# One of the values' four products moves into the ranks' step, and the keys' drain ahead of an exponential

## Chip, cores and metric

One core of a Trainium2 chip. The metric is device time of one execution in microseconds (us), as the median of several runs. TensorE is PE below, VectorE DVE, ScalarE ACT, GpSimd POOL, SyncE SP.

## What is computed

x has 8 x 1024 tokens of 128 features, adj is a 1024 x 1024 mask. All in float32.

```python
# attention layer on y = layernorm(x): 4 heads of 32 features
q, k, v = y @ Wq.T + bq, y @ Wk.T + bk, y @ Wv.T + bv
scores = clip(q @ k / sqrt(32), -10, 10);  scores = where(mask == 0, -10, scores)
# keys stand in 8 chunks of 128; the softmax is taken inside each chunk
ctx = sum over chunks of softmax(scores[chunk]) @ v[chunk]
x = x + (layernorm(ctx @ Wo.T + bo + y) * gamma + beta)
# expert layer: 8 experts, the two best per token, hidden size 256
g = layernorm(x);  best two of (g @ Wg + bg)
out = x + sum over the two of (gelu(g @ W1[e] + b1[e]) @ W2[e] + b2[e])
```

## The kernel before

The tokens are cut into 16 blocks of 512 (u = 0 to 15; two blocks make one batch element). A block goes through 8 steps, one for each chunk of 128 keys (j = 0 to 7; s = 8u + j numbers them all, 128 steps). Each engine has its own program, in which the order is written out by hand; semaphores join them.

In each step PE makes the scores of the chunk for the 4 heads (`scores`, L455: 32 rows of the array for each head, into four PSUM banks, which are there once only), then the context and the sums of the exponentials of the chunk two steps back (`context`, L467 and L474: 32 columns each), and then at most a few jobs for other blocks. The scores wait for the semaphore `clipped` of the step before, as the clip on DVE (`clip`, L1029) reads the same banks. Behind the clip ACT takes the exponential (`exponentials`, L779) of the whole step, in place in a ring `e` of three buffers, and DVE turns the context (L1037).

The jobs of PE in block u, behind the step's `context`: step 0 transposes of normalised x2 of block u-3 (`turn_xn2`, L515); step 1 its gate (L530) and half of the output projection of block u-2 (`project`, L565 and L566); step 2 the other half; step 3 transposes of normalised x of block u+2 (`turn_xn`, L486); step 4 the keys of u+2 (`keys`, L494, one fp32 product of 128 x 512); step 5 the ranks of the tokens of u-3 among their expert pairs (`rank`, L538 to L554, small bf16 products); step 6 the values of u+2 (`values`, L503, four fp32 products of 128 x 128, one for each tile of 128 tokens); step 7 the queries of u+2 (`queries`, L508). A product in fp32 stands in the trace as two matmul passes. `rank` has work from block 3 on; keys, values and queries of u+2 in these steps from block 1 to block 13 (block 0 has an order of its own). The last two blocks have no such products, and behind block 15 come the experts' tiles, in which ranks (L538 to L554) and expert products (L617, L631, L657) stand side by side on PE.

Keys and values of a block go through the same PSUM bank: `values` writes to it once the keys have been drained (semaphore `k_ready`). The drains are ACT's work. Its order in a block, each behind the exponential of its step: step 0 the transposes of x2 (L866); step 1 normalising x (L784); step 2 squares of the projection (L817); step 3 the transposes of x (L832, L842) and the normalising of the projection (L824); step 4 the drain of the keys (`drain_k`, L848) and sums of x of block u+3 (L800); step 5 squares of x (L808); step 6 the drain of the values (`drain_v`, L854); step 7 normalising x2 (L784) and the drain of the queries (L860). The transposes of the next block's step 0 wait for that normalising.

Of the kernel before, what the change touches and what calls it, by code (L numbers as in the profile page):

```python
# [21 lines left out]
TILES = BLOCK // P  # L22
# [58 lines left out]
def need(eng, sem, value):  # L81
    if value > 0:
        eng.wait_ge(sem, value)
# [12 lines left out]
def is_block(u):  # L96
    return 0 <= u < BLOCKS


def done(u):  # L100

    return min(max(u + 1, 0), BLOCKS)


def graph_transformer_layer(nc, x, adjT, wqT, bq, wkT, bk, wvT, bv, wo, bo, gamma, beta,
                            wg, bg, w1, b1T, w2, b2, out):
    ctx = ExitStack()
    with ctx:
# [3 lines left out]
        def sem(name):  # L112
            return ctx.enter_context(nc.semaphore(name))
# [129 lines left out]
        def v_ps(v):  # L243
            return job_ps[1] if v == 1 else job_ps[0]
# [70 lines left out]
        v_filled, v_ready = sem("v_filled"), sem("v_ready")  # L315
# [129 lines left out]
        def _(pe):  # L445
# [48 lines left out]
                pe.matmul(k_ps(v)[:], w_proj[:, W_K, :], xnT[:, v % 2, :], start=True, stop=True)\  # L494
                    .then_inc(k_filled, 1)

            def values(v):
                pe.wait_ge(k_ready, v + 1)
                if v == 0:
                    pe.wait_ge(xnT_bo_ready, 1)  # L500
                for t in range(TILES):
                    cols = slice(t * P, (t + 1) * P)
                    ins = pe.matmul(v_ps(v)[:, cols], xnT[:, v % 2, cols], w_proj[:, W_V, :], start=True, stop=True)  # L503
                ins.then_inc(v_filled, 1)

            def queries(v):
                need(pe, v_ready, v + 1 if v else 0)
# [26 lines left out]
            def rank(v):  # L534
                pe.wait_ge(one_hot_ready, v + 1)
                need(pe, n2_ready, done(v + 1))
                to = job_ps[1][:, 0:(TILES + 1) * NP].rearrange("p (t n) -> p t n", n=NP)
                pe.matmul(to[:, 0:TILES, :], tri[:], one_hot[:], start=True, stop=False, skip_group_check=True)  # L538
                pe.matmul(to[:, TILES, :], all_ones[:], one_hot[:, TILES - 1, :], start=False, stop=False,
                          skip_group_check=True)  # L540
                for t in range(TILES - 1):
                    pe.matmul(to[:, t + 1:TILES + 1, :], all_ones[:],
                              one_hot[:, t:t + 1, :].to_broadcast([P, TILES - t, NP]),
                              start=False, stop=False, skip_group_check=True)
                if v == 0:
                    pe.wait_ge(ranks_begun, 1)
                for part, n in enumerate((ROOM - 1, 1)):
                    ins = pe.matmul(to[:, 0:TILES, :], all_ones[0:n, :],
                                    first_rows[0:n, part:part + 1, :].to_broadcast([n, TILES, NP]),
                                    start=False, stop=v == 0 and part == 1, skip_group_check=True)  # L550
                if v > 0:
                    for part in range(2):
                        before = totals[:, (v - 1) % 2, part:part + 1, :]
                        ins = pe.matmul(to[:], all_ones[0:1, :], before.to_broadcast([1, TILES + 1, NP]),  # L554
                                        start=False, stop=part == 1, skip_group_check=True)
                ins.then_inc(rank_filled, 1)
# [124 lines left out]
            for u in range(BLOCKS):  # L681
                for j in range(CHUNKS):
                    s = u * CHUNKS + j
                    scores(s)
                    if s == LAG:
                        pe.wait_ge(consts_ready, 1)
                    if s >= LAG:
                        context(s - LAG)
                    if u == 0:
                        if j == 0:  # L690
                            values(0)
                            keep_busy(7, ctx_ps[:, 0:P])
                        if j == 1:
                            turn_xn(1)
                            keep_busy(6, ctx_ps[:, 0:P])
                        if j == 2:
                            keys(1)
                        if j == 3:
                            turn_xn(2)
                        if j == 4:  # L700
                            values(1)
                        if j == 5:
                            keys(2)
                            queries(1)
                        if j == 6:
                            values(2)
                        if j == 7:
                            queries(2)
                    last = u == LAST
                    if j == 0 and is_block(u - 3):  # L710
                        turn_xn2(u - 3)
                    if last and j == 0:
                        columns(0)
                    if j == 1 and is_block(u - 3):
                        gate(u - 3)
                    if j in (1, 2) and is_block(u - 2):
                        project(u - 2, range(2 * j - 2, 2 * j))
                    if j == 3 and u > 0 and is_block(u + 2):
                        turn_xn(u + 2)
                    if j == 4 and u > 0 and is_block(u + 2):  # L720
                        keys(u + 2)
                    if j == 6 and u > 0 and is_block(u + 2):
                        values(u + 2)
                    if j == 7 and u > 0 and is_block(u + 2):
                        queries(u + 2)
                    if j == 5 and is_block(u - 3):
                        rank(u - 3)
                    if u == LATE and j == 3:
                        offset_columns()
                    if last and j == 3:  # L730
                        ends(0)
                    if last and j == 7:
                        lookup(0)
# [41 lines left out]
        def _(act):  # L775
            def exponentials(s):
                act.wait_ge(clipped, s + 1)
                every = e[:, s % E_RING]
                nc.scalar.activation(every, every, ACT.Exp, scale=SCORE_SCALE).then_inc(exp_done, 1)  # L779
# [65 lines left out]
            def drain_k(v):  # L845
                act.wait_ge(k_filled, v + 1)
                need(act, clipped, CHUNKS * 2 * (v // 2 - 1))
                nc.scalar.activation(kT[v // 2 % 2][:, v % 2 * BLOCK:(v % 2 + 1) * BLOCK], k_ps(v)[:], ACT.Identity,  # L848
                                     bias=bk_sb[:, 0:1]).then_inc(k_ready, 1)
# [68 lines left out]
            for u in range(BLOCKS):  # L918
                for j in range(CHUNKS):
                    s = u * CHUNKS + j  # L920
                    exponentials(s)
                    if u == 0:
                        if j == 1:
                            drain_xnT(1)
                        if j == 2:
                            drain_k(1)
                            normalise_x(2)
                        if j == 3:
                            drain_xnT(2)
                        if j == 4:  # L930
                            drain_v(1)
                        if j == 5:
                            drain_k(2)
                            drain_q(1)
                        if j == 6:
                            drain_v(2)
                        if j == 7:
                            drain_q(2)
                    if j == 0 and is_block(u - 3):
                        drain_xn2T(u - 3)  # L940
                    if j == 1 and u > 0 and is_block(u + 2):
                        normalise_x(u + 2)
                    if j == 2 and is_block(u - 2):
                        square_proj(u - 2)
                    if j == 3 and u > 0 and is_block(u + 2):
                        drain_xnT(u + 2)
                    if j == 3 and is_block(u - 2):
                        normalise_proj(u - 2)
                    if j == 4 and u > 0 and is_block(u + 2):
                        drain_k(u + 2)  # L950
                    if j == 4 and is_block(u + 3):
                        sum_x(u + 3)
                    if j == 5 and is_block(u + 3):
                        square_x(u + 3)
                    if j == 6 and u > 0 and is_block(u + 2):
                        drain_v(u + 2)
                    if j == 7 and is_block(u - 2):
                        normalise_x2(u - 2)
                    if j == 7 and u > 0 and is_block(u + 2):
                        drain_q(u + 2)  # L960
# [676 lines left out]
```

## Time and profile before

| | |
|---|---|
| median of 3 runs | 727.55 us (727.47 to 728.11) |
| profiled execution | 729.22 us, span 727.5 us from first to last instruction |
| granted TensorE clock, mean | 0.992 |
| busy share of the span | PE 95%, PE weight load 50%, DVE 81%, ACT 74%, POOL 78% |
| costliest lines | exponential L779 245.1 us, clip L1029 293.2 us, sums L474 133.3 us |

How to read it: PE and its weight loads are pipelined, and the ends of matmuls are modelled, so starts are the firmer numbers; a busy PE is not PE at its peak. Times in rows are from the start of the span. The chain is the work that ended last, followed back from the last instruction, each step to what released it.

### The profile page before, as it was taken

What the parts mean: (1) busy time and instruction counts of PE and PEld (TensorE: products, weight loads), DVE (VectorE), ACT (ScalarE), POOL (GpSimd) and SP (SyncE); (2) the same over time, 40 slices, a digit from 0 to 9 for tenths busy, and PEclk for the clock granted to TensorE, in tenths of its full rate; (3) what the DMA queues carried; (4) which work ended last, traced back from release to release, by engine and by line L of the source; (5) the groups of instructions that cost most, each with busy time, mean ns of one, the idle gap of its engine ahead of it and who ended that gap; (6) DMA issues with size and microseconds to landing.
All of it is one profiled execution on the core that took longest, in us unless ns stands there. A gap on an engine that the chain in (4) does not pass through costs nothing.

```text
span 727.5 us, 17325 instructions
## 1 busy us (share of the span) xinstructions
PE 689.7 (95%) x5510; PEld 364.0 (50%) x5510; DVE 590.7 (81%) x1270; ACT 538.6 (74%) x1225; POOL 564.9 (78%) x627
## 2 busy tenths in 40 slices
PE   8997999999999999999999999989888999999994
PEld 6421333333333333333333333323378899999994
DVE  4789989898999989999998999999897655555552
ACT  4776787888878788887888887666676566667662
POOL 7759696989889898988988889898776776545553
PEclk9999999999999999999999999999999999999997
DMA  7450010010100101111010010013241354333300
GB/s 259 157 167 30 1 30 15 17 45 30 45 34 27 45 15 45 45 31 45 16 45 23 27 43 15 30 54 108 62 130 55 97 157 125 97 96 102 105 26 2
DMA packets 47961, 45.45 MB, mean 62 GB/s; under 512 B 6981, under 2 KB 42576, under 8 KB 47872
## 3 DMA queue, kind: packets, MB, share of 16 engines
q1 hardware_dynamic: 41888, 31.60, 15.5%
q0 software_dynamic: 5984, 12.74, 5.0%
q8 instruction: 47, 0.77, 0.5%
q14 instruction: 42, 0.34, 0.2%
HBM read 27.73 MB, written 18.34 MB: 63 GB/s over the span
## 4 chain that ended last, share of the span: by engine, by line
PE 69%; DVE 15%; issue 6%; ACT 5%; DMA 1%; DVEq 1%; SPq 1%; POOLq 0%; POOL 0%; ACTq 0%
PE scores_ps L455 15%; PE ctx_ps L467 11%; DVE e L1029 10%; PE scores_ps L631 9%; PE z_ps L474 9%; PE ctx_ps L657 5%; PE z_ps L657 5%; ACT x_rows L784 3%; PE job_ps L503 2%; PE job_ps L530 2%; PE job_ps L494 2%; PE job_ps L566 2%; ACT e L779 1%; PE job_ps L515 1%; PE job_ps L565 1%
## 5 line engine op out<-in xcount | busy, mean ns | idle before, releaser
L779 ACT ACTIVATE e<-e 128x2048 f32<-128x2048 f32 x128 | 245.1, 1915 | 109.3 <-DVE e L1029 108.5
L1029 DVE SCALAR_TENSOR_TENSOR e<-scores_ps,bound_mem 128x2048 f32<-128x2048 f32 x128 | 293.2, 2290 | 40.0 <-PE scores_ps L455 34.6
L901 ACT ACTIVATE e<-scores_ps,bound_mem 128x128 f32<-128x128 f32 x364 | 104.4, 374 | 51.0 <-PE scores_ps L631 51.0
L1533 POOL DMA_INDIRECT out<-e,near x91 | 91.0, 1000 | 62.0 <-DVE e L1253 49.0
L474 PE MATMUL z_ps<-e,one_column 128*32 128x512 f32 x1024 | 133.3, 592 | 0.0
L1514 POOL TENSOR_TENSOR ctx_part<-ctx_part,z_inv 128x1024 f32<-128x1024 f32 x60 | 115.5, 1925 | 18.2 <-DVE z_inv L1045 18.1
L1526 POOL TENSOR_TENSOR ctx_sum<-ctx_sum,ctx_part 128x512 f32<-128x512 f32 x90 | 115.7, 1285 | 8.4 <-POOL ctx_sum L1526 0.9
L631 PE MATMUL scores_ps<-e,bound_mem 128*128 128x128 f32 x728 | 97.0, 276 | 4.0 <-ACT e L872 2.1
L1037 DVE STREAM_TRANSPOSE ctx_part<-ctx_ps 128x512 f32<-128x512 f32 x128 | 90.3, 705 | 1.6 <-PE ctx_ps L467 1.6
L631 PEld LDWEIGHTS scores_ps<-e,bound_mem 128*128 128x128 f32 x728 | 88.5, 192 | 5.6 <-ACT e L872 3.9
L1488 POOL DMA_INDIRECT sorted_rows<-x_rows,slot x64 | 63.5, 993 | 19.3 <-issue 16.1
L474 PEld LDWEIGHTS z_ps<-e,one_column 128*32 128x32 f32 x1024 | 33.4, 110 | 76.5 <-issue 76.2
L467 PE MATMUL ctx_ps<-e,v_last 128*32 128x512 f32 x512 | 68.2, 604 | 1.4 <-DVE ctx_part L1037 1.3
L467 PE MATMUL ctx_ps<-e,near 128*32 128x512 f32 x512 | 68.2, 605 | 0.0
L1236 DVE TENSOR_TENSOR bound_mem<-near,b_pair 128x128 f32<-128x128 f32 x91 | 28.8, 316 | 41.9 <-issue 40.2
L455 PE MATMUL scores_ps<-near 32*128 32x512 f32 x320 | 45.6, 639 | 4.9 <-DVE e L1029 4.5
L657 PE MATMUL ctx_ps<-bound_mem,e 128*128 x368 | 48.9, 275 | 0.5 <-DVE e L1253 0.5
L455 PE MATMUL scores_ps<-near,k_last 32*128 32x512 f32 x320 | 45.6, 639 | 3.8 <-DVE e L1029 3.4
L657 PE MATMUL z_ps<-bound_mem,e 128*128 x360 | 47.7, 275 | 1.1 <-DVE e L1253 1.1
L657 PEld LDWEIGHTS ctx_ps<-bound_mem,e 128*128 128x128 f32 x368 | 44.8, 192 | 0.8 <-issue 0.7
L657 PEld LDWEIGHTS z_ps<-bound_mem,e 128*128 128x128 f32 x360 | 43.8, 192 | 1.4 <-issue 1.3
L1227 DVE COPY bound_mem<-bound_mem 128x258 f32 x170 | 43.4, 298 | 0.2 <-issue 0.2
(194 smaller groups left out, 1055.8 us busy)
## 6 DMA issues: line engine op xcount, KB each, us to landing
near<-sorted_rows SPq DMA_DIRECT2D x91, 130.0 KB, 2.2
near<-in_x SPq DMA_DIRECT2D x16, 256.0 KB, 2.8
bound_mem<-in_adjT SPq DMA_DIRECT2D x4, 1024.0 KB, 10.0
x_post<-in_x SPq DMA_DIRECT2D x16, 256.0 KB, 2.7
sorted_rows<-pad_row SPq DMA_DIRECT2D x1, 3640.0 KB, 15.3
out<-e,near POOLq DMA_INDIRECT x91, 2.3
sorted_rows<-x_rows,slot POOLq DMA_INDIRECT x64
bound_mem<-in_w SPq DMA_DIRECT2D x1, 1024.0 KB, 5.7
```

The lines of the kernel that those rows point to most:

```text
L455: ins = pe.matmul(scores_ps[:, h, :], kT[u // 2 % 2][rows_of, j * P:(j + 1) * P], qT[u % 3][rows_of, :], start=True, stop=True)
L467: ins = pe.matmul(ctx_ps[rows_of, :], v_sb[u // 2 % 2][:, j, rows_of], e[:, s % E_RING, h, :], start=True, stop=True)
L474: ins = pe.matmul(z_ps[rows_of, :], one_column[:, j, :], e[:, s % E_RING, h, :], start=j == 0, stop=j == CHUNKS - 1, skip_group_check=True)
L631: ins = pe.matmul(scores_ps[:, i % 2, k * P:(k + 1) * P], part_flat[:, at:at + P], xT, start=True, stop=True)
L657: ins = pe.matmul(to, e_flat[:, h_at:h_at + P], w_out[:, bass.ds(ways_out[i][k // 2], D)], start=k == 0, stop=k == 3)
L779: nc.scalar.activation(every, every, ACT.Exp, scale=SCORE_SCALE).then_inc(exp_done, 1)
L901: nc.scalar.activation(e_flat[:, h_at:h_at + P], scores_ps[:, i % 2, k * P:(k + 1) * P], ACT.Gelu, bias=part_flat[:, bias_at:bias_at + 1]) ...
L1029: dve.scalar_tensor_tensor(out=e[:, s % E_RING], in0=scores_ps[:], scalar=-CLIP, in1=to, op0=ALU.max, op1=ALU.min).then_inc(clipped, 1)
L1037: dve.transpose(ctx_part[:, s % PARTS, :, :].rearrange("p a b -> p (a b)"), ctx_ps[:])\
L1514: nc.gpsimd.tensor_tensor(pair, pair, z_inv[:, v % 2, j:j + 2].to_broadcast([P, 2, SQUARES, DH]), ALU.mult).then_inc(ctx_scaled, 1)
L1526: nc.gpsimd.tensor_tensor(to, first, ctx_part[:, at], ALU.add).then_inc(ctx_added, 1)
L1533: nc.gpsimd.indirect_dma_start(out=out_rows, out_offset=bass.IndirectOffsetOnAxis(ap=near_u[:, id_at:id_at + 1], axis=0), in_=e_flat[:, at ...
```

## The change

On PE `values` gets a list of tiles. The product of the first tile of block u+2 is made in step 5, behind the ranks of block u-3 (in blocks 1 and 2, which have no ranks there, behind the step's sums); the other three stay in step 6, and the last of them signals `v_filled` as before. Both groups begin with the wait for `k_ready`. On ACT the drain of the keys of u+2 is put ahead of the exponential of step 4, where it stood behind it. Blocks 1 to 13 are touched.

```diff
-            def values(v):
+            def values(v, tiles=range(TILES)):
                 pe.wait_ge(k_ready, v + 1)
                 if v == 0:
                     pe.wait_ge(xnT_bo_ready, 1)
-                for t in range(TILES):
+                for t in tiles:
                     cols = slice(t * P, (t + 1) * P)
                     ins = pe.matmul(v_ps(v)[:, cols], xnT[:, v % 2, cols], w_proj[:, W_V, :], start=True, stop=True)
-                ins.then_inc(v_filled, 1)
+                if TILES - 1 in tiles:
+                    ins.then_inc(v_filled, 1)
...
                     if j == 6 and u > 0 and is_block(u + 2):
-                        values(u + 2)
+                        values(u + 2, range(1, TILES))
                     if j == 7 and u > 0 and is_block(u + 2):
                         queries(u + 2)
                     if j == 5 and is_block(u - 3):
                         rank(u - 3)
+                    if j == 5 and u > 0 and is_block(u + 2):
+                        values(u + 2, range(1))
...
                     s = u * CHUNKS + j
+                    if j == 4 and u > 0 and is_block(u + 2):
+                        drain_k(u + 2)
                     exponentials(s)
...
-                    if j == 4 and u > 0 and is_block(u + 2):
-                        drain_k(u + 2)
                     if j == 4 and is_block(u + 3):
                         sum_x(u + 3)
```

## Rows read from the trace of the kernel before

**Rows 1.** The page, parts 1 and 4: busy time by engine; the chain by engine.

```profile
PE 689.7 (95%) x5510; PEld 364.0 (50%) x5510; DVE 590.7 (81%) x1270; ACT 538.6 (74%) x1225; POOL 564.9 (78%) x627
...
PE 69%; DVE 15%; issue 6%; ACT 5%; DMA 1%; DVEq 1%; SPq 1%; POOLq 0%; POOL 0%; ACTq 0%
```

**Rows 2.** The chain in block 10, from step 4 on: start us, us, what.

```profile
350.46 1.06 PE job_ps L494 x2
...
355.04 0.12 PE job_ps L554 x2
355.16 1.05 PE scores_ps L455 x8
...
358.06 1.09 PE job_ps L503 x8
...
360.36 2.30 DVE e L1029
...
362.69 0.46 ACT e L779
...
364.50 1.65 ACT x_rows L784 x4
...
366.19 0.66 PE job_ps L515 x4
```

**Rows 3.** Timeline of DVE, block 10, clips of steps 5, 6: start, us, [idle before].

```profile
352.72 2.29 DVE L1029 SCALAR_TENSOR_TENSOR e<-scores_ps,bound_mem 128x2048 f32<-128x2048 f32 x1 [0.70 <-PE scores_ps L455]
...
356.35 2.29 DVE L1029 SCALAR_TENSOR_TENSOR e<-scores_ps,bound_mem 128x2048 f32<-128x2048 f32 x1
```

**Rows 4.** Timeline of PE, last rank matmul and next scores, blocks 10 and 4.

```profile
354.94 0.22 PE L554 MATMUL job_ps<-totals,all_ones 1*128 1x140 bf16 x1
355.07 0.71 PE L455 MATMUL scores_ps<-near,k_last 32*128 32x512 f32 x4
...
166.56 0.22 PE L554 MATMUL job_ps<-totals,all_ones 1*128 1x140 bf16 x1
166.69 0.71 PE L455 MATMUL scores_ps<-near 32*128 32x512 f32 x4
```

**Rows 5.** Timeline of PE, block 10, step 6: sums, values' passes, next scores.

```profile
357.02 1.04 PE L474 MATMUL z_ps<-e,one_column 128*32 128x512 f32 x8
358.00 0.38 PE L503 MATMUL job_ps<-w_proj,near 128*128 128x128 f32 x1
...
358.21 0.50 PE L503 MATMUL job_ps<-w_proj,near 128*128 128x128 f32 x3
...
358.88 0.28 PE L503 MATMUL job_ps<-w_proj,near 128*128 128x128 f32 x1
359.08 0.71 PE L455 MATMUL scores_ps<-near,k_last 32*128 32x512 f32 x4
```

**Rows 6.** Timeline of PE, block 2, step 5: sums, then the next scores.

```profile
102.22 1.04 PE L474 MATMUL z_ps<-e,one_column 128*32 128x512 f32 x8
103.89 1.14 PE L455 MATMUL scores_ps<-near,k_last 32*128 32x512 f32 x8 [0.63 <-DVE e L1029]
```

**Rows 7.** Timeline of PE in the experts' part: rank(13), then an expert product.

```profile
532.45 0.22 PE L554 MATMUL job_ps<-totals,all_ones 1*128 1x140 bf16 x1
532.60 0.38 PE L657 MATMUL z_ps<-bound_mem,e 128*128 x1
...
532.82 0.50 PE L657 MATMUL z_ps<-bound_mem,e 128*128 x3
```

**Rows 8.** Timeline of ACT, block 10, steps 4 to 6: exponentials and the keys' drain.

```profile
351.22 1.95 ACT L779 ACTIVATE e<-e 128x2048 f32<-128x2048 f32 x1
353.02 0.72 ACT L848 ACTIVATE near<-job_ps,bk_sb 128x512 f32<-128x512 f32 x1
...
355.05 1.91 ACT L779 ACTIVATE e<-e 128x2048 f32<-128x2048 f32 x1 [0.15 <-DVE e L1029]
...
358.68 1.91 ACT L779 ACTIVATE e<-e 128x2048 f32<-128x2048 f32 x1 [0.17 <-DVE e L1029]
```

## Prediction, made before the changed kernel was run

> **What bounds the kernel now.** Page first: PE is busy 95% of the span and carries 69% of the chain that ended last, DVE 15%, ACT 5% [rows 1]. All of the edit lies in the 13 blocks u = 1 to 13, so next I read the chain inside one of them (block 10; the others repeat it) [rows 2]. From the keys' product in step 4 to the end of step 6 it stays on PE without a break: scores, context, sums, the step's job, next scores. Only behind the scores of step 7 does it leave PE: clip 2.30 us on DVE, the exponential and the normalising of x2 on ACT, then back to PE for that tile's transposes in the next block's step 0. So whatever moves the scores of step 7 moves the whole next block by the same amount; nothing in the chain between absorbs it.
>
> Then each step was asked what releases its scores: the end of the clip before (scores overwrite the banks that the clip reads) or PE's own queue. In step 5 both come together. The clip runs 352.72 to 355.01 [rows 3]; the next scores start at 355.07, 0.06 after it, and 0.13 after the start of the last rank matmul [rows 4]. Block 4 shows the same 0.13, and so do all the blocks 4 to 13 (in block 3 the records of these two matmuls are missing). In step 6 the clip ends at 356.35 + 2.29 = 358.64 [rows 3], but the next scores start at 359.08 [rows 5]: there PE is the limit, by 0.44 - 0.06 = 0.38 us. Blocks 1 and 2 have no ranks in step 5: in block 2 PE stands idle for 0.63 us until the clip is done [rows 6].
>
> **The change part by part.** No work is added. One product is two fp32 passes; it goes from step 6 to step 5, behind the ranks.
>
> Step 6 loses two passes out of eight. Pass follows pass by (358.88 - 358.21) / 6 = 0.112 us [rows 5]. The group keeps its first pass, which is followed only after 0.21 us, and its last, 0.20 us ahead of the scores. So it gets shorter by 2 x 0.112 = 0.22 us, and the 0.38 us by which PE is later than the clip covers that.
>
> Step 5 in blocks 3 to 13 (11 blocks). The trace of before has no fp32 product of the full array between the ranks and the scores, so I put it together from transitions. Ranks to a full fp32 product: in the experts' part rank(13) is followed by one, 532.45 to 532.60, 0.15 us, and its second pass comes 0.21 us behind its first (532.82) [rows 7]; another pair of this kind has the same two numbers. The same 0.21 us opens the values' own group in step 6, and from its last pass to the scores are 0.20 us (all 15 such groups) [rows 5]. So from the last rank matmul to the scores: 0.15 + 0.21 + 0.205 = 0.57 us where 0.13 stand now. Step 5 grows by 0.44 us, of which 0.22 is the product and 0.22 a price for leaving the ranks' form and coming back. The reading: the ranks' last two matmuls use one row of the array and the scores 32, and they follow each other closely; the product uses 128 rows, so the weights of its first pass, and then those of the scores, are not loaded under running matmuls. In step 6 this price is paid already, behind the sums, and the three products that stay there pay it again.
>
> Bounds of this unknown step: from below, two plain passes with ordinary gaps [rows 5], 0.22, or 0.34 if only the second pass had its weights ahead (0.112 for 0.21); from above 0.44 with nothing hidden. I take 0.44, since the row nearest to it is the very transition from ranks to such a product.
>
> On top of that rests a rule of the Trainium skill, TensorEngine Tiling (Array Packing), Key Properties: changing the tiling mode drains the engine. The rows above agree with it, with some 0.1 us for a change; by that rule the sum is the forecast's, without it that of the plain shift below.
>
> Net on PE: +0.44 - 0.22 = +0.22 us for each of 11 blocks = +2.43 us. The clip of step 6 starts 0.44 later and ends at 359.08; the scores of step 7 now come at 359.08 + 0.22 = 359.30, so PE is still the last there, by 0.16 after the 0.06 of release.
>
> Blocks 1 and 2: the product falls into idle time. Behind the sums a job starts 0.98 us after their first matmul (357.02 to 358.00) [rows 5], so in block 2 at 102.22 + 0.98 = 103.20; plus 0.21 plus 0.20 = 103.61, ahead of the 103.89 that the clip sets [rows 6]. Cost nothing, with 0.28 to spare (in block 1 the idle time is alike); without that cover it would cost what it costs elsewhere. Step 6 gets the 0.22 us shorter: 2 x 0.22 = -0.45 us.
>
> The drain of the keys, ahead of the exponential of step 4 on ACT. Before, that exponential starts at 351.22, the drain at 353.02 [rows 8]. The keys' product ends on PE at 350.46 + 1.06 = 351.52 [rows 2]. So the drain can start at some 351.55, and ACT stands still for some 0.33 us. Behind its wait are queued this exponential (then 352.2 to 354.1), the sums of x, and the next exponential. Their reader on PE is the context product of step 6, at 355.16 + 1.05 = 356.21 [rows 2], now later still: 2 us to spare. ACT had 0.15 us idle ahead of the exponential of step 5 and 0.17 ahead of that of step 6 [rows 8]: the first starts about 0.18 late, the second waits for a clip that is itself 0.44 later. Cost on the path: nothing. Gain: nothing either; the keys are ready at about 352.3 and the product asks for them at 355.1. Even behind the exponential they would be ready at 353.74 (353.02 + 0.72). The new wait of PE on the keys is therefore never the last. SP's and POOL's queues get no instruction more or less, and no DMA moves.
>
> Sum: +2.43 - 0.45 = +1.98 us. The profiled execution took 729.22 us with a span of 727.50; by it 731.2. The median of the three runs is 727.55, so I forecast 727.55 + 1.98 = 729.5 us.
>
> **The rivals.**
> Weights loaded ahead: the queue of PE pulls the second pass's weights under the ranks. Then step 5 grows by 0.34, the net is 0.12 x 11 - 0.45 = +0.9 us, 728.4. For it: within a group weights are loaded under matmuls [rows 5]. Against: the pair in rows 7. Beside this stands the Trainium skill, TensorE: Matmul & The Clock Gate, Part 3, The mechanism: PE pulls a weight load ahead of running matmuls when the row group doesn't conflict or the background buffer is free. By that rule alone this rival would hold; rows 7 show 0.21 instead of 0.112 where it should act.
>
> A plain shift: the product costs 0.22 in step 5, as much as step 6 saves. Only blocks 1 and 2 gain: 727.1 to 727.6.
>
> Room in step 5 (the other side): if PE could take the product before the clip is done there, as in blocks 1 and 2, all 13 blocks would save 0.22: -2.9 us, 724.7. It decides from 0.44 us of idle PE time in step 5. The trace gives 0.13 between the last rank matmul and the scores, and the chain runs through PE there [rows 2, 4]; so hardly.
>
> ACT becomes late: if the 0.33 us of standing still went on through the exponentials into the normalising of x2, less the 0.15 idle, 0.18 x 13 = +2.3 us more, 731.8. Against it: the step's own 2 us to spare, and the later clip of step 6.
>
> That the drain changes nothing by itself is part of the forecast, not a rival.
>
> **How the numbers follow.** Forecast 0.62; weights ahead 0.15; plain shift 0.10; room in step 5 0.07; ACT late 0.06. About 0.2% (1.46 us) is what a measurement of this kernel can tell from no change. The forecast's own range is 729.0 to 730.0 (the upper end without the gain of blocks 1 and 2), nearly all of it slower. Slower: 0.57 of the forecast plus 0.06 = 0.63. Within: 0.05 + 0.15 + 0.10 = 0.30. Faster: 0.07. For 8 in 10 the range takes in the weights-ahead case and the upper part of the plain shift, and above the spread of the runs before (728.11 against 727.55): 727.4 to 730.5.
>
> **What would show it.** In blocks 3 to 13 two passes of the values stand between ranks and scores, the second 0.21 behind the first, and the scores start 0.57 after the last rank matmul and clearly later than 0.06 after the clip; the group of step 6 has six passes and is 0.22 shorter; in blocks 1 and 2 step 5 keeps its length. The drain of the keys stands ahead of the exponential of step 4, which starts some 0.9 us later, with no wait of the context products for ACT. Wrong would be: scores of step 6 still 0.06 behind the clip, a second pass 0.11 behind its first, or context products that wait for exponentials.

## The result, and the profile after

The changed kernel is slower: 730.22 us (median of 9 runs) against 726.55 for the kernel before beside it, ratio 1.0041 with a 95% interval of 1.0031 to 1.0052, so by the ratio some 3.0 us (2.3 to 3.8); the two medians lie 3.7 apart. The forecast was 729.5 us, +2.0 on the 727.55 known then.

The profiled execution of the changed kernel took 729.79 us with a span of 728.1, only 0.6 more than the 727.5 of before. That pair alone would mislead: the two executions differ in their first 60 us, before the change has any effect (below). So first the blocks. The length of each step (from its first scores to the next step's) was compared between the two traces:

```
changed minus before, ns, by step
             j=0   j=1   j=2   j=3   j=4   j=5   j=6   j=7
block 2        3    -1     2     1    -1     0  -223    -1
block 3        1     0     0     2    -3   317  -223    -1
block 4        0     0     2    -2     1   441  -223     0
block 10      -1     1     0     1     0   442  -223     0
block 13       1    -1     2    -2    -3   443  -224     1
```

Blocks 4 to 13 all look like this: step 5 0.44 us longer, step 6 0.22 shorter, the other six unmoved within a few ns. In block 3 step 5 grows by 0.32 only (below). From the start of block 2 to that of block 14 the changed kernel loses 0.75 + 1.28 = 2.03 us (it stood 1.28 ahead of the trace of before at the first and 0.75 behind at the second). The 0.22 us that block 1 gains in step 6 come off this sum; the rest of block 1 is the start-up.

The timeline of PE in the changed kernel, block 10, steps 5 and 6 (start us, us, engine, line, what; lines of PE behind `values` are one higher than before). It answers to [rows 4, 5]:

```profile
354.76 0.28 PE L555 MATMUL job_ps<-totals,all_ones 1*128 1x140 bf16 x2
354.98 0.38 PE L503 MATMUL job_ps<-w_proj,near 128*128 128x128 f32 x1
...
355.19 0.28 PE L503 MATMUL job_ps<-w_proj,near 128*128 128x128 f32 x1
355.39 0.71 PE L455 MATMUL scores_ps<-near,k_last 32*128 32x512 f32 x4
...
357.35 1.04 PE L474 MATMUL z_ps<-e,one_column 128*32 128x512 f32 x8
358.32 0.94 PE L503 MATMUL job_ps<-w_proj,near 128*128 128x128 f32 x6
359.18 1.14 PE L455 MATMUL scores_ps<-near,k_last 32*128 32x512 f32 x8
```

The second of the two rank matmuls starts 0.06 behind the first, at 354.83; the product's passes follow at 354.98 (0.15) and 355.19 (0.21), the scores at 355.39 (0.20). That is 0.57 where 0.13 stood in [rows 4]. The group of step 6 has six passes and is 0.86 us long from its first pass to the scores, where it was 1.08 [rows 5].

The weight loads (PEld) of the same stretch:

```profile
354.97 0.30 PEld L503 LDWEIGHTS job_ps<-w_proj,near 128*128 128x128 f32 x2
355.39 0.20 PEld L455 LDWEIGHTS scores_ps<-near,k_last 32*128 32x128 f32 x4
```

The first load of the product starts together with its pass, and that of the scores together with the scores. Inside the groups of the values a load starts 0.11 us ahead of its pass, in this trace and in that of before. So at both edges of the product the weights were not loaded ahead, as the prediction read it.

DVE, the same steps:

```profile
352.61 2.29 DVE L1032 SCALAR_TENSOR_TENSOR e<-scores_ps,bound_mem 128x2048 f32<-128x2048 f32 x1 [0.70 <-PE scores_ps L455]
...
356.67 2.29 DVE L1032 SCALAR_TENSOR_TENSOR e<-scores_ps,bound_mem 128x2048 f32<-128x2048 f32 x1 [0.40 <-PE scores_ps L455]
```

The clip of step 5 ends at 354.90. In the kernel before, the next scores came 0.06 behind that end; now they come at 355.39, 0.49 behind it: PE is the last. The clip of step 6 had no idle time noted ahead of it [rows 3]; now DVE stands 0.40 us for PE.

ACT, steps 4 to 6, against [rows 8]:

```profile
351.44 0.69 ACT L851 ACTIVATE near<-job_ps,bk_sb 128x512 f32<-128x512 f32 x1 [0.20 <-PE job_ps L494]
352.02 1.90 ACT L782 ACTIVATE e<-e 128x2048 f32<-128x2048 f32 x1
...
354.99 1.90 ACT L782 ACTIVATE e<-e 128x2048 f32<-128x2048 f32 x1
...
359.00 1.91 ACT L782 ACTIVATE e<-e 128x2048 f32<-128x2048 f32 x1 [0.57 <-DVE e L1032]
```

The drain waits 0.20 us for the keys' product, the exponential behind it starts 1.1 us after its clip's end instead of 0.2, and by step 6 ACT waits for the clip again.

**The start.** In the trace of before, block 1 begins 2.4 us later than in that of the changed kernel. And in the changed kernel's profile the granted clock falls in block 1, after PE has stood idle for 2.22 us ahead of the scores of step 3. By stretches of the changed kernel (start and end, length, busy time of PE, PEld, DVE, ACT and POOL, PEclk, DMA share, GB/s):

```profile
58.90:61.00 2.10, 2.04 (x11) 0.53 (x11) 1.36 (x3) 1.91 (x1) 2.10 (x13) 0.50 0.70 210
63.00:80.00 17.00, 16.47 (x124) 5.29 (x120) 15.47 (x14) 13.13 (x25) 16.25 (x12) 1.00 0.00 1
```

```profile
58.96 2.09 PE L455 MATMUL scores_ps<-near 32*128 32x512 f32 x8 [2.22 <-DVE e L1032]
```

PEclk 0.50 is the 1.2 GHz level, 1.00 the 2.4 GHz level. At the lower one these scores take 2.09 us instead of 1.14, and the step 1.38 us more than before. The same idle time in the kernel before has no such fall in its profile; there it came in block 0, at some 20 us. Among the eight profiles taken after the first one, four show it in block 1, one in block 0 and three nowhere ahead of the end, whatever the kernel. From the first scores of the last step to the end of the span all nine profiles agree within 0.4 us (212.5 to 212.9). So what two of these profiles differ by, beyond the effect of the change and those 0.4 us, arises in blocks 0 and 1.

### The profile page after: what moved, and what is told of

The parts are those of the page before. It is cut to its first block, busy times and chain, and to the rows that moved or that the text cites. A ratio compares the mean times of both kernels' runs of the same rounds, so it can differ in the third digit from the quotient of the medians.

```text
span 728.1 us, 17325 instructions
## 1 busy us (share of the span) xinstructions
PE 691.5 (95%) x5510; PEld 363.3 (50%) x5510; DVE 590.0 (81%) x1270; ACT 538.3 (74%) x1225; POOL 565.3 (78%) x627
## 4 chain that ended last, share of the span: by engine, by line
PE 70%; DVE 15%; issue 6%; ACT 5%; DMA 1%; DVEq 1%; SPq 1%; POOLq 0%; POOL 0%; ACTq 0%
PE scores_ps L455 15%; PE ctx_ps L467 11%; PE scores_ps L632 10%; DVE e L1032 10%; PE z_ps L474 9%; PE ctx_ps L658 5%; PE z_ps L658 5%; ACT x_rows L787 3%; PE job_ps L503 2%; PE job_ps L531 2%; PE job_ps L494 2%; PE job_ps L567 2%; PE job_ps L516 1%; PE scores_ps L618 1%; PE job_ps L566 1%
```

## The experiments

Theory A is the prediction's: PE pays for leaving the ranks' form (one row of the array) for the product's (128 rows) and coming back to the scores' (32 rows). B: the moved drain costs something too. C: a product behind the sums costs this much wherever it stands and however many there are.

**The split alone.** The kernel with the values split as in the change, the drain back behind the exponential:

```diff
                     s = u * CHUNKS + j
-                    if j == 4 and u > 0 and is_block(u + 2):
-                        drain_k(u + 2)
                     exponentials(s)
...
+                    if j == 4 and u > 0 and is_block(u + 2):
+                        drain_k(u + 2)
                     if j == 4 and is_block(u + 3):
                         sum_x(u + 3)
```

> The split of the values alone; the drain of the keys stays behind the exponential of step 4. Theory A (a price on PE for leaving the ranks' form and coming back, 0.22 us in each of 11 blocks): step 5 of blocks 4 to 13 is 0.44 us longer than in the kernel before and step 6 0.22 shorter, as in the changed kernel, and the time is the changed kernel's within 0.15%, some 2 to 3 us above before. Rival B (the drain ahead of the exponential costs something too, about the 1 us by which the measured difference exceeds the forecast): 1 us below the changed kernel, about +2.0 us on before.

Measured: 729.3 us against 727.67 beside it, ratio 1.0024 (1.0011 to 1.0036), +1.7 us. In the trace step 5 of blocks 4 to 13 is 0.440 to 0.445 us longer and step 6 0.223 shorter than before: the changed kernel's picture to a few ns. In time alone this result lies nearer to B's +2.0 than to A's 2 to 3 us, with an interval (0.8 to 2.6 us) that reaches into both; it is the steps, and the next run, that decide. By the steps the split alone carries the change.

**The drain alone.** The kernel before with the one move on ACT:

```diff
+                    if j == 4 and u > 0 and is_block(u + 2):
+                        drain_k(u + 2)
                     exponentials(s)
...
-                    if j == 4 and u > 0 and is_block(u + 2):
-                        drain_k(u + 2)
```

> The move of the drain alone; all four products of the values stay in step 6. Theory A: the exponential of step 4 starts some 0.9 us later and nothing on PE moves; steps keep their lengths within 0.01 us, the time is that of before within 0.1%. Rival B: +1 us on before (0.14%), to be seen as steps that are longer or as context products that wait for an exponential.

Measured: 727.76 against 727.67, ratio 1.0000 (0.9987 to 1.0013). No step of blocks 2 to 15 differs by more than 0.01 us from the trace of before, though the exponential of step 4 starts 0.9 us later. Timeline of ACT, block 10:

```profile
348.90 0.69 ACT L848 ACTIVATE near<-job_ps,bk_sb 128x512 f32<-128x512 f32 x1 [0.20 <-PE job_ps L494]
349.48 1.90 ACT L779 ACTIVATE e<-e 128x2048 f32<-128x2048 f32 x1
351.28 0.30 ACT L800 ACTIVATE unused<-near 128x128 f32<-128x128 f32 x1
...
352.45 1.90 ACT L779 ACTIVATE e<-e 128x2048 f32<-128x2048 f32 x1
```

B falls: nothing waits for what the drain pushes back, and, as the split alone shows, nothing needs the keys earlier.

**The product ahead of the ranks.** The changed kernel with two lines exchanged on PE:

```diff
+                    if j == 5 and u > 0 and is_block(u + 2):
+                        values(u + 2, range(1))
                     if j == 5 and is_block(u - 3):
                         rank(u - 3)
-                    if j == 5 and u > 0 and is_block(u + 2):
-                        values(u + 2, range(1))
```

> As the changed kernel, but the product of step 5 stands ahead of the ranks, behind the sums. Theory A: ranks begin with matmuls over the full array too, so no further change of form comes in; what remains is the first pass's 0.21 and 0.11 to the first rank matmul: step 5 grows by 0.32 instead of 0.44 us, each block by 0.10 instead of 0.22, so 1.3 us (0.18%) less than the changed kernel. Rival C (the product costs this wherever it stands in step 5): step 5 +0.44, the changed kernel's time.

Measured: 726.77 against 727.67, ratio 0.9993 (0.9982 to 1.0005): in time this can't be told from the kernel before. Step 5 of blocks 4 to 13 grows by 0.13 us and step 6 shrinks by 0.18: a block is 0.05 shorter, not 0.10 longer. The same product with the same two passes costs 0.31 us less in step 5 for standing before the ranks instead of behind them. So C falls, and A's direction holds; but the growth is smaller than the 0.32 that I put together. Timeline of PE, block 10:

```profile
351.96 0.49 PE L503 MATMUL job_ps<-w_proj,near 128*128 128x128 f32 x2
352.29 0.21 PE L539 MATMUL job_ps<-one_hot,tri 128*128 128x112 bf16 x1
...
352.79 0.22 PE L555 MATMUL job_ps<-totals,all_ones 1*128 1x140 bf16 x1
352.79 0.71 PE L455 MATMUL scores_ps<-near,k_last 32*128 32x512 f32 x3
352.85 0.22 PE L555 MATMUL job_ps<-totals,all_ones 1*128 1x140 bf16 x1
352.91 1.06 PE L455 MATMUL scores_ps<-near,k_last 32*128 32x512 f32 x5
```

The first rank matmul comes 0.33 after the product's first pass, as forecast. But at the other end three matmuls of the scores start at 352.79, together with the last but one of the ranks and ahead of its last at 352.85; the fourth head's starts at 352.91. The ranks' last matmuls use one row; so by these starts they run side by side with the three heads that use other rows of the array (the trace doesn't name the heads, so that it is the head on the same row that waits is a reading). In the kernel before this overlap was there to be had but the clip came later: step 5 had 0.325 - 0.13 = 0.19 us of room on PE. Some 0.04 of it is lost again in step 6, which is 0.18 shorter here and not 0.22: the fourth head starts 0.12 behind the others.

Counted from PE's own pace the price is larger than the 0.22 of the forecast. Without the product behind them the scores can start 0.06 ahead of the last rank matmul (352.79 against 352.85), with it they start 0.57 behind: 0.62 us, of which 0.22 are passes and 0.40 the price. The clip hid 0.18 of that in the kernel before.

The weight loads fit: the first one of the ranks starts under the product's second pass, 0.11 us ahead of its own matmul at 352.29.

```profile
352.18 0.10 PEld L539 LDWEIGHTS job_ps<-one_hot,tri 128*128 128x128 bf16 x1
```

Two other causes drop out with this run. It isn't the change between fp32 and bf16: here a bf16 matmul over 128 rows follows an fp32 pass after 0.11 us, as one fp32 pass follows another, while the ranks' own step from 64 rows to one takes 0.15 within bf16 (354.67 to 354.82 in the kernel before; the one-row matmuls follow each other by 0.06), and 0.21 and 0.20 stand in step 6 between fp32 matmuls [rows 5]. And it isn't the second wait for `k_ready`: the first job behind the sums starts 0.52 us after their last matmul, with that wait ahead of it (`values`) or without (`rank`).

**Two products behind the ranks.** The changed kernel with `range(2)` in step 5 and `range(2, TILES)` in step 6:

```diff
-                        values(u + 2, range(1, TILES))
+                        values(u + 2, range(2, TILES))
...
-                        values(u + 2, range(1))
+                        values(u + 2, range(2))
```

> As the changed kernel, with two of the four products in step 5. Theory A (a price for each change, not for each product): step 5 of blocks 4 to 13 +0.67 us, step 6 -0.39 (the clip then sets its end, by 0.06), a block +0.28; time about +2.3 us on before (11 x 0.28, less 2 x 0.38 in blocks 1 and 2). Rival C (each product costs 0.44 behind the ranks): step 5 +0.89, a block +0.50, +4.7 us on before.

Measured: 730.27 against 727.67, ratio 1.0036 (1.0023 to 1.0050), +2.6 us. Step 5 +0.66 to +0.67, step 6 -0.39, a block +0.28. Timeline of PE, block 10:

```profile
356.34 0.28 PE L555 MATMUL job_ps<-totals,all_ones 1*128 1x140 bf16 x2
356.55 0.71 PE L503 MATMUL job_ps<-w_proj,near 128*128 128x128 f32 x4
357.19 1.14 PE L455 MATMUL scores_ps<-near,k_last 32*128 32x512 f32 x8
```

The second product adds 0.22 us, two plain passes; the price on top of the first (another 0.22 beyond the clip) is paid once for the group, not for each product. Rival C's 0.89 for step 5 is out.

**The changed kernel again.** The same kernel as was predicted, unchanged.

> The changed kernel once more, beside more runs of before. Theory A: the blocks add up to +1.98 us (11 x 0.22, less 2 x 0.22), and what the first comparison showed beyond it (+3.0) comes from the first 60 us, which differ from execution to execution whatever the kernel; so +2.0 to +2.6 us on before in time, and +0.22 in each of blocks 4 to 13 again. If a real further cost is there, +3 us again, with a place in the trace that is longer in every profile of the changed kernel.

Measured: 729.99 against 727.17, ratio 1.0043 (1.0026 to 1.0061), +2.8 us by the medians and 3.1 by the ratio. In the blocks +0.22 each again (step 5 0.441 to 0.444). This profile has no fall of the clock in its first 700 us, like that of the drain alone, in which PE does just what it does in the kernel before. These two begin block 1 within 0.07 us of each other. At the first scores of the last block they stand 1.95 us farther apart, and that is the blocks' own sum: 10 x 0.22 + 0.09 in block 3, less 2 x 0.22 in blocks 1 and 2, plus 0.10 that step 7 of block 1 gives back. Their spans are 1.8 us apart.

The times are less clear. This run missed its forecast of 2.0 to 2.6 by a little, on the side of the +3 of a further cost. The fastest executions are 2.4 us apart here, 2.1 for the split alone, but 3.0 in the first comparison (729.24 against 726.20). Taken together, the 27 executions of the changed kernel (both times) and of the split alone average 2.4 us (1.9 to 2.8) more than the 65 of the kernel before beside them; the blocks' 1.95 lies within that, 3.0 doesn't. No stretch of the profiles of the changed kernel behind block 2 holds more than the +0.22 of each block. That what the first comparison showed beyond this is how its executions began is what the profiles point to; a systematic part of some tenths of a us isn't excluded.

**Blocks 1 and 2 alone.** The kernel before with two products in step 5 where there are no ranks (`values` takes a list of tiles, as in the change):

```diff
                     if j == 6 and u > 0 and is_block(u + 2):
-                        values(u + 2)
+                        values(u + 2, range(2 if u < 3 else 0, TILES))
...
+                    if j == 5 and 0 < u < 3:
+                        values(u + 2, range(2))
```

> Only blocks 1 and 2, which have no ranks in step 5, get products there, two each; blocks 3 to 13 and the drain are as in the kernel before. Theory A: the two products hide in the idle time of step 5 (length unchanged), step 6 is 0.38 us shorter (then the clip sets its end): -0.76 us on before, 0.1%. If PE's price for coming back from such products holds there too, step 5 of blocks 1 and 2 is longer and nothing is gained.

Measured: 727.21 against 727.17, ratio 1.0003 (0.9994 to 1.0012): in time this can't be told from no change, and the forecast of -0.76 us lies outside the interval (-0.4 to +0.9). In the trace of block 2 step 5 keeps its length and step 6 is 0.387 us shorter, as forecast; in block 1 step 6 is 0.36 shorter, though step 3 of that block carries the fall of the clock in this profile (+1.55), so that block can't be read as a whole. In the run with two products, whose profile has no such fall in block 1, that block's step 7 gives 0.24 of its 0.36 back: there the clip, behind DVE's own work, ends at 80.89 and the scores follow at 81.03. The forecast left this out; by the steps some -0.5 us are to be had.

**Both.** The product ahead of the ranks in blocks 3 to 13, two products in blocks 1 and 2, against the changed kernel:

```diff
-                        values(u + 2, range(1, TILES))
+                        values(u + 2, range(2 if u < 3 else 1, TILES))
...
+                    if j == 5 and u > 0 and is_block(u + 2):
+                        values(u + 2, range(2 if u < 3 else 1))
                     if j == 5 and is_block(u - 3):
                         rank(u - 3)
-                    if j == 5 and u > 0 and is_block(u + 2):
-                        values(u + 2, range(1))
```

> The product ahead of the ranks in blocks 3 to 13, two products in step 5 in blocks 1 and 2. Theory A, with the sizes of the run with the product ahead of the ranks: 11 x -0.05 and 2 x -0.38 = -1.3 us on before (-0.18%), the fastest of all; step 5 of blocks 4 to 13 +0.13, step 6 -0.18.

Measured: 725.8 us against 727.17, ratio 0.9984 (0.9973 to 0.9995), -1.2 us. Step 5 +0.13 and step 6 -0.18 in blocks 4 to 13, step 6 of block 2 -0.39. It beats both kernels, the one before by 0.16% and the changed one, taken beside it, by 0.6%. In block 2 the two products stand in the time in which PE was idle [rows 6]:

```profile
100.37 1.04 PE L474 MATMUL z_ps<-e,one_column 128*32 128x512 f32 x8
101.34 0.71 PE L503 MATMUL job_ps<-w_proj,near 128*128 128x128 f32 x4
102.04 1.14 PE L455 MATMUL scores_ps<-near,k_last 32*128 32x512 f32 x8
```

## Why the prediction was right, point by point

- *PE is the chain through steps 4 to 7, nothing behind absorbs a shift of the scores of step 7.* Right: six of eight steps keep their lengths, and each block's +0.22 is still there at block 14.
- *Step 6 gets 0.22 shorter, covered by the 0.38 that PE is later than the clip.* Right: 0.223. With two products it is 0.39 and no more, as the clip then sets the end: the bound was real.
- *Step 5 grows by 0.44, put together from 0.15, 0.21 and 0.20 of three other places.* Right in ten blocks: 0.15, 0.21, 0.20 and 0.442. In block 3 it is 0.32. The prediction says that the records of its last two rank matmuls are missing there; in truth `rank` makes none for the first block of tokens (L551), its ranks end earlier, and PE had that much more room ahead of the clip. This makes the sum 0.13 us smaller. The 0.15 was from the experts' part of the same trace, in which ranks already stood ahead of an fp32 product.
- *The reading behind it: a price for each change of form.* It stands: one product more costs 0.22, the plain passes, the same product ahead of the ranks costs 0.13, and the loads at both edges of the product start with the work that needs them. The Trainium skill's rule (TensorEngine Tiling (Array Packing), Key Properties) that a change of tiling mode drains the engine agrees with these rows. The rival by which the second pass's weights are loaded under the ranks fails: the second pass comes 0.21 behind the first.
- *In step 5 clip and PE come together.* This step was wrong, without harm to the sum. I took the 0.13 between the last rank matmul and the scores for PE's own pace. It was the clip's: PE can run the ranks' last matmuls beside the scores and had 0.19 us of room. Room that only work ahead of the ranks can use, since a product behind them stands between the two and forbids the overlap; that is why the rival with room in step 5 failed for this change, and why the exchange of two lines takes 0.31 us off step 5 of the changed kernel. The price of 0.22 is what was left of 0.40 beyond the clip; that the sum was right all the same is due to counting from where the scores stood, whatever held them there.
- *Blocks 1 and 2 hide the product.* Right in block 2 (step 5 +0.00, step 6 -0.22), where PE still idles 0.21 us behind the product. In block 1 the profile of the changed kernel is overlaid by the start; in its second profile step 5 is unchanged and step 6 -0.22 too, but step 7 gives 0.10 back, which the prediction didn't see.
- *The drain's move costs and gains nothing.* Right: 1.0000. The drain began where forecast, 0.03 us behind the end of the keys' product, and the exponential of step 5 came 0.06 us late where 0.18 was forecast; step 6 waits for the clip.
- *+1.98 us.* The blocks give 1.95, as two profiles that begin alike show, and all executions together 2.4 (1.9 to 2.8). That 1.95 comes so near is in part luck: block 3 takes 0.13 off the forecast sum and step 7 of block 1 adds 0.10. Luck also helped the time itself. The first comparison showed 3.0 by the ratio, a half more than forecast, and 730.22 us stayed below the upper end of 730.5 because the kernel before, at 726.55, ran 1.0 faster beside it than the 727.55 from which the forecast counted. The term that was too small is not one of the change's steps but the scatter of the executions: I had put 0.56 us for it, from three runs, and executions of one and the same kernel spread over 4.2 us (726.15 to 730.35 for the kernel before).

## What to carry to other kernels

Before a small matmul is moved into a gap on PE, look at what stands to either side: a product over other rows of the array than its neighbours costs a change on each side on top of its passes (here 0.40 us on 0.22, of which another engine's wait hid 0.18), and its place in the order decides whether that is paid. A gap of PE that another engine's release ends is not PE's pace; its room shows only when something is put there. And a steady effect in a loop is read best step by step from two traces: here 0.22 us of 31 was plain there, while the times of whole executions scattered by more than the whole effect.

## What the runs showed of the hardware that was not expected

- By their recorded starts, matmuls of different rows of the array pass each other: with the product ahead of the ranks, three heads of the scores start at 352.79, 0.06 us ahead of the ranks' last matmul, which stands before them in the program; the fourth starts at 352.91. The Trainium skill, TensorE: Matmul & The Clock Gate, Part 3, The mechanism, has matmuls of different tiles side by side but start in program order; by their recorded starts these did not.
- The sums of x on ACT were faster behind an exponential than behind the keys' drain: 0.30 us a piece in blocks 2 to 12 where it was 0.34 to 0.35. The drain alone isn't the cause: in block 1 of the kernel before they stood behind it too and took 0.30. What is, no run shows. It gave ACT back a part of its wait, and no time.
- The granted clock falls for a moment in block 0, in block 1 or not at all, from execution to execution; in block 1, behind 2.22 us of idle PE, it made its step 1.4 to 1.6 us longer, of which the next step gave 0.3 back.
